# Making the experts stage's first routing inside the scan stage's last two chunks

## The reference, cut to what matters

```python
# layer 1, attention: a selective scan, D_INNER 512, N_STATE 16
u   = silu(conv(x_in));  dt = softplus(dt_in @ dt_proj_w.T + dt_proj_b)
h   = exp(dt * A) * h + (dt * u) * B          # token after token, 512 x 16 states
y   = (sum_n h * C + u * D_param) * silu(res)
x   = layernorm(x + y @ out_proj_w.T)
# layer 1, ffn: 8 heads of 32, 16 experts of inner size 128, the best 2 per head and token
t    = (x @ Wm + bm).reshape(4096 * 8, 32)
w    = softmax(t @ expert_emb);  topw, topi = top_k(w, 2)
eo   = gelu(t @ W1 + b1) @ W2 + b2            # all 16 experts are computed
out  = sum over the two chosen of topw * eo
x    = layernorm(x + out @ Wo + bo)
```

## Time and profile before

| | us |
|---|---|
| median of 3 runs | 3373.77 |
| their range | 3370.49 to 3374.05 |
| the profiled execution's time | 3369.65 |
| its span, first to last instruction | 3367.9 |
| VectorE busy | 2653.4 (79%) |
| TensorE busy, multiplying | 3023.6 (90%) |
| ScalarE busy | 2226.0 (66%) |
| GpSimd busy | 2217.1 (66%) |

### The profile page before, as it was taken

The page is one execution under the profiler, slowest core; times in us unless marked ns, Lnnn a source line. Parts: engine busy times, 40 slices in busy tenths (PEclk is TensorE's granted clock), DMA queues, the critical chain, the costliest instruction groups (busy, mean ns, idle before and its releaser), DMA issues. The chain is left out here.

```text
span 3367.9 us, 39358 instructions
## 1 busy us (share of the span) xinstructions
PE 3023.6 (90%) x11504; PEld 1717.0 (51%) x11504; DVE 2653.4 (79%) x3525; ACT 2226.0 (66%) x3402; POOL 2217.1 (66%) x1611
## 2 busy tenths in 40 slices
PE   3589999999999999999889999999977799999997
PEld 1157666667666667776334433443433344444443
DVE  5989999898989898554799999999997545555543
ACT  2457676767767666665566566566653688888887
POOL 3578888888888888775467776776774244444444
PEclk7689999999999999999999999999988899999999
DMA  3034444444444444554122222222222122222222
GB/s 97 13 95 133 125 129 128 119 136 121 127 129 126 127 119 130 145 146 125 58 72 71 71 72 70 72 71 70 71 72 66 63 99 99 105 105 105 106 105 94
DMA packets 199617, 335.38 MB, mean 100 GB/s; under 512 B 21379, under 2 KB 57380, under 8 KB 199020
## 3 DMA queue, kind: packets, MB, share of 16 engines
q1 hardware_dynamic: 199404, 332.86, 32.5%
HBM read 325.69 MB, written 7.09 MB: 99 GB/s over the span
## 5 line engine op out<-in xcount | busy, mean ns | idle before, releaser
L1366 POOL TENSOR_TENSOR c_hc<-c_h,c_c_rep 128x1024 f32<-128x1024 f32 x256 | 604.3, 2361 | 284.7 <-DVE c_h L1405 228.9
L1405 DVE TENSOR_TENSOR_SCAN c_h<-c_decay,c_carry,c_v_ps 128x512 f32<-128x512 f32 x512 | 632.7, 1275 | 0.5 <-DVE c_v_ps L1395 0.5
L1882 POOL TENSOR_TENSOR d_acc<-d_acc,d_prod 128x512 f32<-128x512 f32 x240 | 310.6, 1309 | 448.8 <-DVE d_prod L1950 448.7
L1287 ACT ACTIVATE c_decay<-c_dt,c_a_cols 128x512 f32<-128x512 f32 x512 | 364.3, 720 | 356.5 <-DVE c_h L1405 355.1
L1840 ACT ACTIVATE d_hmid<-d_up,d_b 128x1024 f32<-128x1024 f32 x512 | 532.0, 1118 | 76.1 <-PE d_up L1735 75.9
L1154 PE MATMUL c_y_ps<-c_hc,ident 128*128 128x512 f32 x1024 | 504.7, 617 | 44.7 <-POOL c_hc L1366 29.9
L687 POOL TENSOR_TENSOR ab_inner_low<-ab_inner,ab_inner_high 128x512 fp32r<-128x512 f32 x264 | 341.8, 1295 | 241.2 <-ACT ab_inner_high L570 239.9
L559 ACT ACTIVATE ab_gate_ps<-ab_gate_ps,ab_raw_d 128x512 f32<-128x512 f32 x264 | 174.6, 661 | 431.0 <-PE ab_gate_ps L414 430.8
L669 POOL TENSOR_TENSOR ab_hc<-ab_h,ab_c_rep 128x512 f32<-128x512 f32 x256 | 331.5, 1295 | 86.8 <-DVE ab_h L740 65.1
L1950 DVE SCALAR_TENSOR_TENSOR d_prod<-d_ring,d_b,d_w_rep 128x512 f32<-128x512 f32 x240 | 180.1, 751 | 245.0 <-PE d_ring L1745 192.6
L1735 PE MATMUL d_up<-d_heads,d_w 128*128 128x512 f32 x1024 | 328.5, 438 | 19.7 <-ACT d_hmid L1840 19.7
(11 more groups left out here) (228 smaller groups left out, 6305.1 us busy)
## 6 DMA issues: line engine op xcount, KB each, us to landing
ab_raw_gu<-in_b_experts SPq DMA_DIRECT2D x264, 256.0 KB, 3.4
ab_w_rep<-ab_w_scratch SPq DMA_DIRECT2D x264, 256.0 KB, 3.6
c_c_rep<-c_c_scratch SPq DMA_DIRECT2D x256, 256.0 KB, 3.1
d_w_rep<-d_w_scratch SPq DMA_DIRECT2D x256, 256.0 KB
ab_raw_d<-in_b_experts SPq DMA_DIRECT2D x264, 129.0 KB, 2.1
ab_raw_x<-in_xT SPq DMA_DIRECT2D x32, 256.0 KB, 4.8
out<-xT SPq DMA_DIRECT2D x8, 512.0 KB, 5.8
xT<-in_xT SPq DMA_DIRECT2D x1, 3072.0 KB, 12.6
```

The source lines that it names most:

```text
L1287: nc.scalar.activation(decay[:, i % DEC, :], dt[:, s, m, :], ACT.Exp, scale=a_cols[:, n * NM + m:n * NM + m + 1]).then_inc(decay_ready, 1)
L1366: nc.gpsimd.tensor_tensor(hc[:, q % HC], h[:, q % HR], c_rep[:, q % BC].unsqueeze(1).broadcast_to([P, PAIR, CH]), ALU.mult).then_inc(hc_re ...
L1405: nc.vector.tensor_tensor_scan(out=h[:, q % HR, m, :], data0=decay[:, i % DEC, :], data1=v_ps[m][:], initial=carry[:, i:i + 1], op0=ALU.mu ...
L1882: nc.gpsimd.tensor_tensor(acc[:, s, g, :], acc[:, s, g, :], prod[:, q % PR, :], ALU.add).then_inc(add_ready, 1)
```

## The change

The first routing of the experts stage, and the making of its weights, move into the scan stage. A new class `FirstRouting` holds both.

SyncE issues nine small loads (`load_vectors`) at the start of the scan block, and two large ones (`load_matrices`: the selection matrices, 512 KB, and W1, 1024 KB) in chunk 6 at q = 15, once the last convolution has read `xin` and `conv_diag`, whose memory they take. `place_embedding` runs on VectorE ahead of the scan loop. In chunk 6 ScalarE rounds both matrices (q = 18, 21), and GpSimd subtracts for the low parts of W1 in four pieces (q = 21, 23, 25, 27). In chunk 7, in the steps where the earlier chunks make the next inputs, TensorE projects (q = 0, 1), spreads eight heads (q = 7 to 14) and makes the logits (q = 17); ScalarE makes the high parts (q = 5, 6) and keeps heads (q = 10 to 17) and logits (q = 20); VectorE makes the two low parts (q = 5, 6). The turn, the eleven steps, the exponential, the turn back and the store stand behind the last scan, among `skip` and `residual`. `project_out` of chunk 6 goes two steps later in chunk 7, with its residuals. For the last chunk, half 1 of `project_out` gets a bank of its own (`v_ps[0]`), and its first two products stand ahead of the second gate. `dtu` has one buffer instead of two. The tiles `u`, `dt`, `conv_diag`, `xin` are placed last, so that the new tiles can overlie them and stay through to the experts stage. There the loads, `split_weights` and the routing of chunk 0 are gone, and the semaphores are set to the counts that they would have reached.

The diff, cut to its core:

```diff
+class FirstRouting:
...
+        self.raw = placed("raw", [P, E * self.INNER], at_xin)
+        self.sel_raw = placed("sel_raw", [P, HPG, 2, P], at_diag)
+        self.w1 = placed("w1", [P, E, self.INNER], at_diag, F32R)
+        self.parts = placed("parts", [P, GROUPS, 2, CH], at_xin, F32R)
+        self.heads_low = placed("heads_low", [P, 4, CH], at_dt, F32R)
+        self.heads_high = placed("heads_high", [P, 4, CH], at_u, F32R)
...
+    def load_matrices(self, sp):
+        sp.dma_start(self.sel_raw[:], self.w["sel"]).then_inc(self.matrices_loaded, 16)
+        sp.dma_start(self.raw[:], self.w["w1"].rearrange("p e i -> p (e i)")).then_inc(self.matrices_loaded, 16)
+
+    def store_weights(self, sp):
+        sp.wait_ge(self.wt_ready, 1)
+        sp.dma_start(self.w_dram[0].rearrange("g j e t -> (g j e) t"), self.w_t[:]).then_inc(self.w_stored, 16)
+        sp.wait_ge(self.w_stored, 16)
...
+    def spread_head(self, pe, i, bank):
+        if i < 2:
+            pe.wait_ge(self.low_ready, i + 1)
+        else:
+            pe.wait_ge(self.head_ready, i - 1)
+        pe.wait_ge(self.low_ready, i // self.HPG + 1)
...
+    def round_sel(self, act):
+        act.wait_ge(self.matrices_loaded, 2 * 16)
+        self.nc.scalar.copy(self.sel[:], self.sel_raw[:]).then_inc(self.sel_ready, 1)
+
+    def round_w1(self, act):
+        act.wait_ge(self.sel_ready, 1)
+        self.nc.scalar.copy(self.w1[:], self.raw[:].rearrange("p (e i) -> p e i", e=self.E)
+                            ).then_inc(self.w1_ready, 1)
...
+    def low_parts(self, pool, n):
+        nc, rows = self.nc, slice((1, 3)[n // 2] * self.DH, ((1, 3)[n // 2] + 1) * self.DH)
+        half = slice(n % 2 * 8, n % 2 * 8 + 8)
+        pool.wait_ge(self.w1_ready, n + 1)
+        nc.gpsimd.tensor_tensor(self.w1[rows, half], self.raw[rows].rearrange("p (e i) -> p e i", e=self.E)[:, half],
+                                self.w1[rows, half].bitcast(F32), ALU.subtract).then_inc(self.w1_ready, 1)
+        pool.wait_ge(self.w1_ready, n + 2)
...
@@ layer1_scan, SyncE
+                    if q == 15 and c == NCH - 2:
+                        sp.wait_ge(cv_ready, NCH * NM)
+                        nx.load_matrices(sp)
+
+            nx.load_vectors(sp)
             store_c(0, 0)
             over_chunks(sp, NCH, chunk)
+            nx.store_weights(sp)
...
@@ layer1_scan, TensorE
+                    else:
+                        if q < 2:
+                            if q == 0:
+                                pe.wait_ge(gp_left, c * NM)
+                            else:
+                                pe.wait_ge(scaled, c * 2)
+                            nx.project(pe, xT, q, (bank_a, bank_b)[q])
+                        elif 7 <= q < 15:
+                            nx.spread_head(pe, q - 7, (bank_a, bank_b)[(q - 7) % 2])
+                        elif q == 17:
+                            nx.project_logits(pe, bank_b)
...
             over_chunks(pe, NCH, chunk)
+            pe.wait_ge(v_ready, NCH * NT - PAIR)
+            nx.turn_logits(pe, k["ident"], b_ps[0])
             add_states(NCH - 1, NU - 2)
             add_states(NCH - 1, NU - 1)
-            project_out(NCH - 1, 0, (0, 1, 2, 3), True)
-            project_out(NCH - 1, 1, (0, 1, 2, 3), True)
+            pe.wait_ge(h_ready, NCH * NT - 1 + DEC)
+            project_out(NCH - 1, 0, (0, 1), True)
+            project_out(NCH - 1, 1, (0, 1), True)
+            project_out(NCH - 1, 0, (2, 3), True)
+            pe.wait_ge(v_ready, NCH * NT)
+            nx.turn_weights(pe, k["ident"], b_ps[1])
+            project_out(NCH - 1, 1, (2, 3), True)
...
@@ layer1_scan, ScalarE
+                    if c == NCH - 2 and q == 18:
+                        nx.round_sel(act)
+                    if c == NCH - 2 and q == 21:
+                        nx.round_w1(act)
+                    if last:
+                        if q in (5, 6):
+                            nx.high(act, q - 5, (bank_a, bank_b)[q - 5])
+                        elif 10 <= q < 18:
...
+                            nx.keep_head(act, q - 10, (bank_a, bank_b)[q % 2])
+                        elif q == 20:
+                            nx.keep_logits(act, bank_b)
...
             activate_gate(NCH - 1)
+            nx.exp(act)
+            nx.keep_weights(act, b_ps[1])
...
@@ layer1_scan, GpSimd
+                    if c == NCH - 2 and q in (21, 23, 25, 27):
+                        pool.wait_ge(hc_ready, c * NU + q + 1 + HR)
+                        nx.low_parts(pool, (q - 21) // 2)
...
@@ layer1_scan, VectorE
+                    if last and q in (5, 6):
+                        nx.low(dve, q - 5, (bank_a, bank_b)[q - 5])
...
+            nx.place_embedding(dve)
             first_input()
             over_chunks(dve, NCH, chunk)
+            nx.route_max(dve, b_ps[0])
+            for n in range(3):
+                nx.route_pick(dve, n)
             skip(NCH - 1, 1, 1)
+            for n in range(3, 7):
+                nx.route_pick(dve, n)
             residual(NCH - 1, 0)
             residual(NCH - 1, 1)
...
@@ layer1_experts
-            store_weights(0, 0)
             over_chunks(sp, NCH, chunk)
...
-            split_weights(0)
-            low(0, 0)
...
-            route_max(0)
-            for n in range(PICKS):
-                route_pick(0, n)
+            dve.sem_inc(route, ROUTE)
+            dve.sem_inc(picked, 1)
             over_chunks(dve, NCH, chunk)
```

## The result

The changed kernel takes **3345.61 us** (median of 4 runs, 3343.66 to 3351.18), the kernel before beside it 3373.08 (4 runs, 3370.49 to 3374.05): ratio **0.9923, 95% interval 0.9909 to 0.9937**. That is 27.5 us faster. The forecast was 42.5 us, and the time lies 4.6 us above the end of the range. The span of the profiled execution went from 3367.9 to 3343.5 us.

A forecast was written before the change was run, and what follows sets the result against it. VectorE was taken to bound the scan stage, with poor stretches of 17.5 and 41.3 us behind it. First gelu -42.1, weights' stream -1.9 and VectorE +1.5 gave -42.5: 3331.3 us against the median 3373.8, range 3325 to 3341.

The forecast's parts named there:

- the weights' stream: Experts stage: first `w_rep` 44.0 us earlier, 1.9 more than the gelus, so chunk 1 waits less: -1.9, bounds 0 and -2.7.
- steps of the experts' chunks above 91: Sign that the forecast is wrong; first high parts were expected 86.7 and near 90 us apart.
- Rival 5: Scan stage: tiles lie elsewhere, VectorE's instructions take longer, kernel slower, 3374 us and more; chance 0.03.
- +1.5: VectorE in chunk 7 of the scan stage: two `low` at 0.751 us each added to a stream without gaps.
- First gelu: Start of the experts stage: with the old stretch gone, first gelu at 2599.0 instead of 2641.10, -42.1 us.
- The tail, price 0: Behind the last scan: added routing steps leave the block's end where it was; 0 us, bounds -1.5 and +4.
- The meeting with GpSimd's gates: Scan stage's tail: VectorE steps with two SBUF inputs wait for GpSimd's gate, ending 0.55 us behind it.
- The last thing is the store: Sign expected in the profile after: the store of the weights comes last in the scan block, done at 2597.4.
- Rival 4: TensorE stays at 2.4 GHz across the boundary into the experts stage: -1 to -4 us, 3327 to 3330; chance 0.09.
- The covered parts: Scan stage: placing, loads, roundings, GpSimd's pieces (2.36 us each), TensorE's products and `keep_head` fit into idle time; 0 us.
- Rivals 1, 2 and 6: 1: added work reaches VectorE, 3-12 us (0.17 with 6); 2: tail longer, 2-4 (0.10); 6: first `up` waits elsewhere, under 10.

The follow-up runs named there:

- e1_pad64: Changed kernel with one unused 64-byte tile per partition ahead of the experts stage's tiles (`w_rep` at remainder 96): 3328.26 us, ratio 0.9873.
- e3_pad224: Changed kernel with an unused 224-byte tile ahead of the experts stage's tiles (`w_rep` at a multiple of 256): 3323.84 us, ratio 0.9858.
- e7_before_pad160: Kernel before the change with 160 unused bytes ahead of the experts' tiles (`w_rep` at remainder 0): 3364.34 us, ratio 0.9977.
- e2_before_pad192: Kernel before the change with 192 unused bytes ahead of the experts stage's tiles (`w_rep` at remainder 32): 3389.67 us, ratio 1.0053.
- e11_half1_old_bank: Changed kernel with 224 bytes of padding, half 1 of the last `project_out` back in `bank_a` behind the first residual: 3324.55 us (one run).
- e12_before_own_bank: Kernel before with 160 bytes of padding, plus only the new order and own bank for half 1 of the last `project_out`: 3360.89 us (one run).

## Why the prediction was wrong

**The step that failed is the weights' stream.** It carried the 88.12 us from one chunk's first `w_rep` to the next over to the changed kernel and asked only when the stream would start. It measured 90.04 for the first chunk and 90.43 on average, above TensorE's 89, so the transfers bound the stage. That gave back 15.3 us over seven chunks. In the forecast's own terms: the first gelu came 41.2 us earlier and the end only 24.4, so everything behind the first gelu is 16.8 longer, where the term said -1.9 with bounds of 0 and -2.7. The list of what would show it wrong had the right mark (steps of the experts' chunks above 91): the second is 92.73, from these rows of ScalarE, which answer to the earlier trace rows.

```profile
2693.03 0.69 ACT L2070 ACTIVATE d_parts<-d_ring,n_heads_b 128x512 fp32r<-128x512 f32 x1
...
2785.76 0.69 ACT L2070 ACTIVATE d_parts<-d_ring,n_heads_b 128x512 fp32r<-128x512 f32 x1
```

**Rival 5 had the right suspicion and the wrong victim.** It said that tiles lie elsewhere now, and then asked only whether VectorE's instructions mind; it looked at the scan stage's tiles only, too. What minded was a DMA into a tile of the experts stage. The scan stage's `c_rep` went from 96 past 256 to 32 past 256 as well (155232 to 97824); there VectorE sets the pace with transfers to spare, and the scan loop shows nothing of it: 958.15 us against 956.52, where +1.5 was forecast. (Single scans are recorded as 2% longer, a median of 1298 ns against 1274, and the loop is not.)

**With the start repaired the step holds.** In e1_pad64, which has the old remainder, the second distance of the high parts is 89.31 instead of the earlier trace rows's 91.78: 2.5 of the 2.7 lost are back, forecast 1.9. Like against like the whole change is worth -43.0 (e1_pad64 against before, remainder 96), -40.5 (e3_pad224 against e7_before_pad160, remainder 0; 43 to 46 had been expected) and -44.1 (changed against e2_before_pad192, remainder 32). The last two pairs were not run side by side, and the kernel before beside each read 3371.2 to 3373.1. The forecast was -42.5. From the first `w_rep` to the end the changed kernel is still 1.6 to 3.0 us the longer of each pair; the clock at the end of the span, see below, makes part of that.

**First gelu.** Forecast -42.1 +1.5 = -40.6, measured -41.2. The two `low` took 0.78 each (0.75 priced) and the scan loop 1.6 more; it also began 0.5 earlier (1622.81 against 1623.35), which nobody forecast, so the last scans came 1.1 later and not 1.5.

**The tail, price 0.** Right to a microsecond: the last residual 16.6 behind the last scan instead of 17.4. The meeting with GpSimd's gates came as the earlier trace rows said, 2.15 and 2.34, both ending 0.55 behind the gate. Two things went differently and nearly cancel. The last `add_states` took 1.98 us at a granted clock of 1.00, where it was 3.78 at 0.50, so `skip`'s input was there 4.5 us behind the last scan instead of 6.35. But the steps stood ahead of `skip` on VectorE: it began 1.5 us later than its input, 6.1 behind the last scan, and with it the second gate. What kept the clock up is open: e11_half1_old_bank, without the early products of half 1, had 1.00 too, and e12_before_own_bank, without the routing, 0.99 (2582 to 2597). The last thing is the store, as said, but barely: it was issued at 2595.76, and `w_rep` follows 0.99 behind the last residual, at 2598.54; in e11_half1_old_bank, where the residual comes last, it follows 0.65 behind.

**Rival 4 came in part.** TensorE did not stay at 2.4 GHz (0.50 from 2600 to 2602), but the granted clock right behind the boundary (2598.5 to 2610) is 0.85; before, in its first 11 us (2638.8 to 2650), it was 0.74. The first high part behind the boundary, chunk 1's inputs, came 42.5 earlier than before (2605.93 against 2648.45) where the gelu came 41.2 earlier. That these 1.3 us come from the clock is argued; no run tests it.

**The covered parts cost nothing**, as said. GpSimd's four pieces on 32 partitions took 2357 ns each, so partitions don't count there (the forecast's 2.36):

```profile
L1086 POOL TENSOR_TENSOR n_w<-n_raw,n_w x4: 2351/2357/2363, 2424.6 to 2447.2; 32x1024 fp32r<-32x1024 f32 x4
```

`dtu` of chunk 7 ended at 2456.65, where it had been 2456.97. In the whole scan loop VectorE waited 0.9 us, before 0.7. Rivals 1, 2 and 6 did not come.

## What to carry to other kernels

When a change adds, removes or overlays tiles, compute where every tile that a DMA fills lies before and after, and price its remainder like an instruction; a tile whose own code nobody touched got 2% slower to fill here (4% from best to worst). Where a transfer's pace is near the pace of the engine that it feeds (here 88.1 against 89 us), start its tile at a multiple of 256 bytes or split it: the changed kernel with 224 bytes of padding takes 3323.84 us, 21.8 less than the changed kernel and 1.4% less than the one before. And compare two kernels at the same remainders before judging the change itself.

## What the runs showed of the hardware

The speed of this case's DMA, which writes 128 rows of 2 KB into SBUF, depends on the first byte of the rows, counted from a multiple of 256: 32 of them took 75.3 us at remainder 0, 75.6 at 128, 76.3 at 96, 77.0 at 64, 78.0 at 32 and 78.2 at 224.

The end of the span has some 3 us that come and go with TensorE's clock. The last eight output products took 3.69 us in the changed kernel (2.4 GHz),

```profile
3323.91 3.69 PE d_ring L2013 x8
...
3333.03 1.57 PE d_ring L81 x2
3334.60 1.72 PE d_ring L82 x2
```

and in e1_pad64, at a granted clock of 0.68, they took 5.38:

```profile
3304.92 5.38 PE d_ring L2014 x8
...
3315.74 2.05 PE d_ring L81 x2
3317.78 1.52 PE d_ring L82 x2
```

The granted clock in the small steps was 0.58 in the changed kernel and 0.55 in e1_pad64. Before, the eight took 3.69 and the two small steps 1.10 and 0.87, all at 1.00. What decides it no run shows. It is part of the 3.6 us by which the last chunk and the end are longer after the change; the rest is mostly the last chunk's transfers, 78.38 against 76.26.
